# Slot starts from one product per two batches: two batches' thresholds in one tile, four moving columns, high and low parts added on VectorE

## The reference, cut to what matters

```python
edge_aggr = jnp.zeros((n, 128)).at[row].add(edge_features)       # n = 6250 nodes, 206250 edges
combined = jnp.concatenate([x, edge_aggr, global_expand], axis=-1) @ W_c + b_c
h = softplus(combined @ W1 + b1)
h = softplus(h @ W2 + b2)
out = _layernorm(x + h @ W3 + b3)
```

## Time and profile before

| what | value |
|---|---|
| median of 3 runs | 1718.69 us (1718.37 to 1723.56) |
| the profiled execution | 1720.1 us, its span 1718.3 us |
| counts and tables | 0 to about 62 us |
| main stage, first to last scatter | 67.7 to 1224.6 us |
| members stage and network | to 1718.3 us |
| PE / DVE / ACT / POOL busy, share of the span | 96% / 77% / 62% / 68% |
| granted PE clock, mean | 0.989 of full speed |

### The profile page before, as it was taken

The page is one execution under the profiler, slowest core; times in us unless marked ns, Lnnn a source line. Parts: engine busy times, 40 slices in busy tenths (PEclk is TensorE's granted clock), DMA queues, the critical chain, the costliest instruction groups (busy, mean ns, idle before and its releaser), DMA issues.

```text
span 1718.3 us, 62458 instructions
## 1 busy us (share of the span) xinstructions
PE 1658.1 (96%) x14853; PEld 1573.1 (92%) x14853; DVE 1328.6 (77%) x3884; ACT 1066.1 (62%) x3462; POOL 1166.5 (68%) x1473
## 2 busy tenths in 40 slices
PE   7899999999999999999999999999899999999985
PEld 4699999999999999999999999999799999999953
DVE  7887777777777777777777777777489898899957
ACT  1355555555555555555555555555588888888886
POOL 1477777777777777777777777777555555555536
PEclk9899999999999999999999999999899999999998
DMA  6377778777777787777777887777699999999922
GB/s 165 93 233 238 233 244 255 247 241 237 234 239 239 248 254 248 241 241 232 238 238 248 251 251 240 238 236 240 203 296 304 299 304 297 303 298 302 297 74 72
DMA packets 172834, 412.01 MB, mean 240 GB/s; under 512 B 31283, under 2 KB 46563, under 8 KB 172756
## 3 DMA queue, kind: packets, MB, share of 16 engines
q1 hardware_dynamic: 112956, 259.93, 49.3%
q0 software_dynamic: 52160, 148.16, 26.4%
q10 hardware_dynamic: 7689, 3.60, 1.2%
HBM read 234.52 MB, written 177.03 MB: 240 GB/s over the span
## 4 chain that ended last, share of the span: by engine, by line
PE 84%; DMA 3%; issue 3%; ACT 2%; POOL 2%; POOLq 1%; DVE 1%; SPq 0%; ACTq 0%; DVEq 0%
PE ps L1224 54%; PE ps L1296 21%; PE ps L1182 2%; PE ps L1195 2%; PE ps L1235 1%; DMA arena<-in_feats 1%; PE ps L1186 1%; DMA members<-buckets 1%; POOL buckets L534 1%; ACT arena L1079 1%; ACT arena L1081 1%; DMA buckets<-arena,index 1%; POOL sums L569 1%; DMA buckets<-arena,direct_at 1%; PE ps L1192 1%
## 5 line engine op out<-in xcount | busy, mean ns | idle before, releaser
L1224 PE MATMUL ps<-arena 128*120 128x129 f32 x9084 | 1045.6, 274 | 3.0 <-DVE arena L812 2.4
L1224 PEld LDWEIGHTS ps<-arena 128*120 128x120 f32 x9084 | 1019.8, 183 | 5.6 <-DVE arena L812 3.6
L534 POOL DMA_INDIRECT buckets<-arena,index x757 | 793.1, 1048 | 235.5 <-issue 149.0
L812 DVE TENSOR_SCALAR arena<-slot_no,slot_f 128x360 f32<-128x360 f16 x1514 | 554.1, 419 | 253.4 <-PE ps L1224 226.8
L1023 ACT ACTIVATE arena<-ps 120x387 f32<-120x387 f32 x757 | 373.6, 494 | 370.4 <-PE ps L1224 221.6
L1296 PE MATMUL ps<-mark,members 128*128 128x128 f32 x3648 | 413.4, 276 | 9.8 <-ACT mark L1110 7.2
L1296 PEld LDWEIGHTS ps<-mark,members 128*128 128x128 f32 x3648 | 411.1, 193 | 12.1 <-issue 10.5
L856 DVE TENSOR_SCALAR mark<-node_no,members 128x128 f32<-128x128 f16 x1368 | 363.1, 332 | 57.5 <-DMA members<-buckets 50.3
L569 POOL TENSOR_TENSOR sums<-sums,staged 128x128 f32 x456 | 225.3, 494 | 199.9 <-ACT staged L1098 102.8
L978 ACT ACTIVATE reach<-block_no,arena 128x128 f16<-128x128 f16 x806 | 316.8, 394 | 0.7 <-PE ps L1235 0.7
L1104 ACT ACTIVATE apart<-node_no,members 128x128 f32<-128x128 f16 x456 | 181.0, 397 | 35.4 <-DMA members<-buckets 25.6
(11 more groups left out here) (171 smaller groups left out, 601.7 us busy)
## 6 DMA issues: line engine op xcount, KB each, us to landing
members<-buckets SPq DMA_DIRECT2D x456, 258.0 KB, 3.6
arena<-in_feats SPq DMA_DIRECT2D x201, 516.0 KB
buckets<-sums SPq DMA_DIRECT2D x48, 258.0 KB
buckets<-arena,index POOLq DMA_INDIRECT x757
buckets<-sums SPq DMA_DIRECT2D x49, 129.0 KB
buckets<-sums SPq DMA_DIRECT2D x49, 64.5 KB
xn<-in_x ACTq DMA_DIRECT2D x1, 2800.0 KB
arena<-in_xT SPq DMA_DIRECT2D x11, 250.0 KB, 3.9
```

Of the source, the lines that this page charges most:

```text
L534: pool.indirect_dma_start(units, bass.IndirectOffsetOnAxis(ap=index[0:SLOTS, s, b:b + 1], axis=0), rows[0:SLOTS, o, :], None).then_inc(sca ...
L812: dve.tensor_scalar(perm[0:TP, b, t, :], slot_no[0:TP, :, :].rearrange("p r b -> p (r b)"), slot_f[0:TP, s, b * TPB + t:b * TPB + t + 1], ...
L1224: mm = pe.matmul(ps[0:SLOTS, MOVED + b, r * ROWF:(r + 1) * ROWF], perm[0:TP, b, t, r * SLOTS:(r + 1) * SLOTS], feat[0:TP, s, b * TPB + t, ...
```

## The change

Two batches share one `reach` tile: `border2` is taken from a product that the kernel already made for another table (`PAIRS`), with the even batch's buckets on partitions 0 to 63 and the odd batch's on 64 to 127. `goto16` gets four columns for each pair of batches: even high, even low, odd high, odd low, with zeros in the half that belongs to the other batch. PE makes one product of four columns for each pair, and because high and low parts now lie in different columns, DVE adds them (`sum_gotos`), once for each chunk, between PE and ACT's `indices`. ACT makes one tile for two batches.

```diff
-        goto16 = sb("goto16", [P, JB], f16)
+        goto16 = sb("goto16", [P, HALF, 2, 2], f16)
+        border2 = sb("border2", [P, HALF])
+        goto_f = sb("goto_f", [P, 2, CB])
-        reach = sb("reach", [P, RS, P], f16)
+        reach = sb("reach", [P, RS // 2, P], f16)
# POOL, at the start
+            pool.memset(goto16[:, :, :, :], 0.0).then_inc(goto_zeroed, 1)
# DVE, tables: one 51-column subtraction instead of two, and one memset more
+                dve.memset(tri_at16[:, ODD + KS:ODD + KS + 1], float(P)).then_inc(tables16_set, 1)
# DVE, before the loop
-            for h, part in enumerate(halves(goto16)):
-                rise = ps[:, RISE + h, 0:HALF]
-                dve.wait_ge(rise_done, h + 1)
-                dve.tensor_scalar(part, rise, 0.125, None, ALU.mult).then_inc(goto_a, 1)
-                dve.wait_ge(goto_a, 2 * h + 1)
-                dve.scalar_tensor_tensor(part[ODD:P, :], rise[ODD:P, :], 0.125, part[ODD:P, :], ALU.mult, ALU.subtract)\
-                   .then_inc(goto_a, 1)
+            rise = ps[:, RISE, 0:HALF]
+            dve.wait_ge(goto_zeroed, 1)
+            dve.wait_ge(rise_done, 1)
+            for odd in range(2):
+                own = slice(odd * ODD, (odd + 1) * ODD)
+                dve.tensor_scalar(goto16[own, :, odd, 0], rise[own, :], 0.125, None, ALU.mult).then_inc(goto_a, 1)
+            dve.wait_ge(goto_a, 2)
+            for odd in range(2):
+                own = slice(odd * ODD, (odd + 1) * ODD)
+                dve.scalar_tensor_tensor(goto16[own, :, odd, 1], rise[own, :], 0.125, goto16[own, :, odd, 0],
+                                         ALU.mult, ALU.subtract).then_inc(goto_a, 1)
+
+            def sum_gotos(c, s):
+                n = CB if not isinstance(c, int) else chunk_batches(c)
+                dve.wait_ge(reach_used, c * (CB // 2) + n // 2)
+                wait(dve, index_ready, c - 1)
+                dve.tensor_reduce(goto_f[0:SLOTS, s % 2, 0:n],
+                                  ps[0:SLOTS, GOTO + s % 2, 0:2 * n].rearrange("p (b h) -> p b h", h=2), AX.X, ALU.add)\
+                   .then_inc(goto_summed, 1)
...
             permutation(0, 0)
+            sum_gotos(0, 0)
             permutation(0, 1)
# DVE, in place(), behind the permutation
+                if b == 0 and (not last or c + 1 < CHUNKS):
+                    sum_gotos(c + 1, s + 1)
# ACT, before the loop
+            act.activation(border2[:, :], ps[:, PAIRS, 0:HALF], ACT.Copy, scale=-1.0, bias=0.5).then_inc(border2_made, 1)
# ACT, reached()
-                wait(act, reach_used, g + 1 - RS)
+                wait(act, reach_used, j + 1 - RS // 2)
-                act.activation(reach[:, r, :], block_no[:, :], ACT.Sign, bias=border[:, bass.ds(g, 1)])\
+                act.activation(reach[:, r, :], block_no[:, :], ACT.Sign, bias=border2[:, bass.ds(j, 1)])\
# ACT, indices()
-                act.wait_ge(reach_used, c * CB + n)
+                act.wait_ge(goto_summed, c + 1)
-                act.activation(index[0:SLOTS, s, 0:n], ps[0:SLOTS, GOTO + s % 2, 0:n], ACT.Identity,
+                act.activation(index[0:SLOTS, s, 0:n], goto_f[0:SLOTS, s % 2, 0:n], ACT.Identity,
# ACT, take()
-                if not ends or k + AHEAD < NBAT:
-                    reached(i * BODY + (k + AHEAD), (k + AHEAD) % RS)
+                if k % 2 == 1 and (not ends or k + AHEAD < NBAT):
+                    reached(i * (BODY // 2) + (k + AHEAD) // 2, (k + AHEAD) // 2 % (RS // 2))
# PE, before the loop: both products into one PSUM bank, DVE is told after the second
-            for h, part in enumerate(halves(count_f)):
-                pe.matmul(ps[:, RISE + h, 0:HALF], differ[0:KS, :], part[0:KS, :], start=True, stop=True)\
-                  .then_inc(rise_done, 1)
+            for odd in range(2):
+                at_ = (1 - odd) * ODD
+                mm = pe.matmul(ps[:, RISE, 0:HALF], differ[0:KS, at_:at_ + P],
+                               count_f[0:KS, :].rearrange("p (j a) -> p j a", a=2)[:, :, odd], start=(odd == 0), stop=(odd == 1))
+            mm.then_inc(rise_done, 1)
# PE, gotos()
-                wait(pe, index_ready, c - 1)
-                pe.wait_ge(reach_made, c * CB + nb)
-                for b in range(nb):
-                    pe.matmul(ps[:, GOTO + s % 2, b:b + 1], reach[:, (s * CB + b) % RS, :],
-                              goto16[:, bass.ds(c * CB + b, 1)], start=True, stop=True).then_inc(reach_used, 1)
+                wait(pe, goto_summed, c - 1)
+                pe.wait_ge(reach_made, c * (CB // 2) + nb // 2)
+                for j in range(nb // 2):
+                    pe.matmul(ps[:, GOTO + s % 2, 4 * j:4 * j + 4], reach[:, (s * (CB // 2) + j) % (RS // 2), :],
+                              goto16[:, bass.ds(c * (CB // 2) + j, 1), :, :].rearrange("p j a h -> p (j a h)"),
+                              start=True, stop=True).then_inc(reach_used, 1)
```

More of the change, by code:

```diff
@@ L55, in gnn_bucketed_edge_sum_mlp_layernorm @@
     assert (TP * TPB + K * (ROWS - 1)) // ROWS <= SLOTS <= P and ROWS * ROWF <= 512
-    assert ROWS == 3
+    assert ROWS == 3 and CB % 2 == 0 and NBAT % 2 == 0 and AHEAD % 2 == 1
     MS = 8
@@ L122, in gnn_bucketed_edge_sum_mlp_layernorm @@
         ones32 = sb("ones32", [P, P])
-        differ = sb("differ", [P, P])
+        differ = sb("differ", [P, ODD + P])
         before16 = sb("before16", [P, P], f16)
@@ L270, in gnn_bucketed_edge_sum_mlp_layernorm @@
         goto_a = sem("goto_a")
+        goto_zeroed = sem("goto_zeroed")
+        border2_made = sem("border2_made")
+        goto_summed = sem("goto_summed")
         starts_made = sem("starts_made")
@@ L626, in masks @@
                 dve.tensor_copy(tri_at16[:, ODD:ODD + KS], tri[:, 0:KS]).then_inc(tables16_set, 1)
+                dve.memset(tri_at16[:, ODD + KS:ODD + KS + 1], float(P)).then_inc(tables16_set, 1)
+                dve.tensor_tensor(differ[:, ODD:ODD + KS + 1], eye[:, 0:KS + 1], ident[:, 0:KS + 1], ALU.subtract)\
+                   .then_inc(tables16_set, 1)
                 dve.tensor_copy(ident2_16[0:K, 0, :], eye[0:K, 0:K]).then_inc(tables16_set, 1)
@@ L634, in masks @@
                     dve.memset(before16[:, at_ + KS:at_ + KS + 1], float(P)).then_inc(tables16_set, 1)
-                    dve.tensor_tensor(differ[:, at_:at_ + KS + 1], eye[:, 0:KS + 1], ident[:, 0:KS + 1], ALU.subtract)\
-                       .then_inc(tables16_set, 1)
             def mark_bucket(k):
@@ L972, in _, with reached @@
                .then_inc(boff1_made, 1)
-            def reached(g, r):
-                wait(act, reach_used, g + 1 - RS)
-                if not isinstance(g, int):
+            act.activation(border2[:, :], ps[:, PAIRS, 0:HALF], ACT.Copy, scale=-1.0, bias=0.5).then_inc(border2_made, 1)
+            def reached(j, r):
+                wait(act, reach_used, j + 1 - RS // 2)
+                if not isinstance(j, int):
                     act.nop(nofuse=True)
-                act.activation(reach[:, r, :], block_no[:, :], ACT.Sign, bias=border[:, bass.ds(g, 1)])\
+                act.activation(reach[:, r, :], block_no[:, :], ACT.Sign, bias=border2[:, bass.ds(j, 1)])\
                    .then_inc(reach_made, 1)
@@ L988, in indices @@
                         act.wait_ge(scattered[STREAMS - 1], 16 + body * 16)
-                act.activation(index[0:SLOTS, s, 0:n], ps[0:SLOTS, GOTO + s % 2, 0:n], ACT.Identity,
+                act.activation(index[0:SLOTS, s, 0:n], goto_f[0:SLOTS, s % 2, 0:n], ACT.Identity,
                                scale=4.0 * RUNITS, bias=part_row[0:SLOTS, :]).then_inc(index_ready, 1)
-            act.wait_ge(border_made, 2)
+            act.wait_ge(border2_made, 1)
             act.wait_ge(iota_set, 7)
-            for g in range(RS):
-                reached(g, g % RS)
+            for j in range(RS // 2):
+                reached(j, j)
             act.wait_ge(ends_done, 1)
@@ L1027, in _ @@
                 set_locals(0, c)
-            for g in range(RS, AHEAD):
-                reached(g, g % RS)
+            for j in range(RS // 2, (AHEAD + 1) // 2):
+                reached(j, j % (RS // 2))
             indices(0, 0, 0, 0)
```

## The result

The changed kernel takes 1730.16 us (median of 4 runs, 1729.12 to 1731.74) against 1719.91 us for the kernel before over 4 runs (1718.37 to 1723.56). The ratio is 1.0055, with a 95% interval of 1.0043 to 1.0067: 0.55% slower, and 2 us beyond the upper end of the range. The profiled execution took 1731.7 us, its span is 1729.1 us against 1718.3.

What follows compares the result with a forecast made beforehand. The prediction took POOL's back-to-back scatters, 22.93 us a body, to bound the main stage; +0.7 before the loop and -0.8 in the first bodies made -0.1 us, 1718.6 us. The range was 1706 to 1728 us.

Steps and rivals of the forecast that it cites:

- PE's saving: Main stage: 403 fewer products and weight loads save PE 0.16 us a body, nothing of the span, since POOL hides it.
- The sum: Main stage, DVE: 202 new sums of 0.2 us, 40 us in all, fit inside its waits for PE; nothing on the path.
- Rivals A and D: Main stage: A (0.10), PE sets the pace, 1686 to 1711; D (0.02), POOL waits for `index` at each chunk, 1800.
- POOL makes descriptors without a pause: Main stage: POOL's idle 0.305 us per instruction is a step, not a wait, so POOL paces bodies at 22.93 us.
- POOL's durations: Main stage: scatter times vary with DVE's phase, bounds -24 to +23 us; first bodies give -0.8, the rest is 0.
- rival C: Main stage: POOL is disturbed more, collisions of 0.53 us repeat; one in every second body adds 12, 1731 us; chance 0.16.
- The gain of 0.8: First three bodies of 138.23 to 207.83 us: PE catches up sooner and saves their excess, -0.8 us.
- ACT's order: Main stage: a chunk's last tile is made behind the row copy before the one it used to follow; worth nothing by itself.
- The companion claim: Main stage: with ACT's tile made sooner, PE no longer waits for `reach` ahead of its own next move; worth nothing.
- Before the loop: Start, DVE's four `goto16` steps: +1.0 us, +3.3 if strided writes double them; +0.7 taken into the sum.
- One memset at the start ... Nothing: Start, POOL: the added memset runs while POOL has nothing else to do and costs nothing.
- rivals B and C: Overlap of lines 812 and 534: B (0.19), POOL disturbed less, 1707 us; C (0.16), disturbed more, 1731 us.

Runs made afterwards that it cites:

- early_before: The kernel before with ACT making each `reach` tile one batch earlier (AHEAD 12 in place of 11); 1727.91 us, ratio 1.0033.
- keys_after: The changed kernel with the bucket numbers that `hot` compares against read from PSUM in place of SBUF; 1710.88 us, ratio 0.9946.
- sum_before: The kernel before with a DVE reduce of the products' bank added per chunk, result unused, ACT's `indices` waiting for it; 1720.32 us, ratio 0.9991.
- late_reach: The changed kernel with the shared `reach` tiles made one batch later, a chunk's last tile again behind the row copy; 1719.78 us, ratio 0.9993.
- keys_before: The kernel before with the bucket numbers that `hot` compares against read from PSUM in place of SBUF; 1701.36 us, ratio 0.9899.
- all_fixed: start_fixed with the bucket numbers that `hot` compares against read from PSUM; 1704.53 us, ratio 0.9896 to the kernel before.
- fixed_late: all_fixed with the shared tiles made one batch later, as in late_reach; 1707.04 us, ratio 0.9911 to the kernel before.
- fixed_pe_load: all_fixed with every slot product issued twice, the second into unused columns; 1696.77 us, ratio 0.9864 to the kernel before.
- fixed_both_load: all_fixed with every slot product issued twice and an extra unread ACT tile in even batches; 1698.57 us, ratio 0.9863 to the kernel before.
- zero_act: The changed kernel with `goto16` cleared by ACT in place of POOL's memset; 1731.43 us, ratio 1.0063 to the kernel before.
- start_fixed: The changed kernel with `goto16` cleared by ACT and stored in four planes, so DVE writes without gaps; 1728.75 us, ratio 1.0055.

## Why the prediction was wrong

**Right.** PE's saving (0.20 us a body, forecast 0.16) is hidden behind POOL: POOL's idle time is 0.305 us per instruction after as before, and nothing above 0.32 is found past 130 us. The 403 tiles fewer on ACT gain nothing by themselves. The sum is hidden; it takes 0.16 us, forecast 0.2. Members stage and network are unchanged. Rivals A and D didn't happen: POOL's pace is slower than PE's, and ACT's `index` is never late. "POOL makes descriptors without a pause" is right as far as the pause goes; what POOL does in that time no run shows. For the direct scatters of the kernel before the trace has 1.007 us of POOL each and 2.4 us (median) from issue to landing.

**The step that failed is POOL's durations**, "More I can't derive, so the rest is 0". It put the change of the scatters' durations at nothing; it was 6.5 us. The place was known in part and the outcome was written down as rival C: a repeated collision at 0.53 us, of which ten more pass the 5.2 us that count as slower. Twenty more came, 20 x 0.53 = 10.6 us; all `hot`s together took 9.5 us more from POOL and the other DMAs some 3 less. I gave C a chance of 0.16 and took no part of it into the sum. The gain of 0.8 that I expected in the first bodies was a loss instead: from the first scatter to the third body the kernel after lost another 1.1 us (4.0 to 5.0). No run isolates that part.

**Behind it, ACT's order**, "Worth nothing by itself". It was seen (the last tile moves from behind a row copy to before the one it used to follow) and costed by the work alone, with the reason that POOL sets the pace. But where POOL is disturbed depends on DVE's phase (scatters over 1.5 us had their `hot` 0.09 to 0.13 us in), and a step moved on an engine with slack shifted that phase here. early_before shows that this alone brings 38 collisions in place of 17 and costs 6 to 7.5 us in a kernel with nothing else changed. The companion claim, that PE then no longer waits for `reach`, is false as well: 12.3 us against 1.6, inside PE's slack.

**Before the loop** is the other term that failed, by size: +0.7 in the sum, +4.0 at the first scatter. For the four steps the forecast was +1.0 and the bound for strided writes +3.3. The steps start 62.11 - 60.84 = 1.27 later and take 4.32 us where before 62.07 - 60.84 = 1.23 were left on the path, in all 4.4 at the first permutation (66.43 against 62.07). The forecast had 2.22 for the four steps. Stored without gaps they take 2.43, so the chain was costed rightly and the value between the bounds was chosen wrongly: the doubling came. Of the later start, "One memset at the start ... Nothing" is the cause on average: POOL had nothing else to do, but DVE had, and 1.31 us of its first step went to the memset. I asked what POOL's path would lose, and not whom the instruction would hold. PE's clock moved along with the start, as the forecast took it: the granted clock is 0.50 from 62 to 72 us in the kernel after, 0.87 from 72 to 76 and 1.00 after, before 0.50 from 62 to 68, 0.87 from 68 to 70 and 1.00 after. By an estimate from these shares it reached 1.00 near 73.0 us, before near 68.5. Nothing of the delay came back by it.

**The reading of the earlier trace rows was wrong too.** I took the scatter's end, 0.15 us after the permutation pair, as a sign that the pair holds POOL. The pair only stands next to `hot` in DVE's order, and the place that rivals B and C name, line 812 beside line 534, is the wrong one. In the timeline of the kernel after, from 994.4 to 996 us, VectorE has nothing to do behind `hot`:

```profile
994.41 1.55 POOL L540 DMA_INDIRECT buckets<-arena,index  x1 [0.30 <-ACT arena L1048]
994.52 0.56 DVE L653 TENSOR_TENSOR hotc<-keys_k,arena 128x392 f16<-128x392 f16 x1
995.96 0.41 DVE L832 TENSOR_SCALAR arena<-slot_no,slot_f 128x360 f32<-128x360 f16 x1 [0.88 <-PE ps L1251]
```

The scatter takes 1.55 us all the same, with the next permutation only at its end; and keys_after leaves every pair in place and has no scatter above 1.19. So the scatters of 1.5 us and more go with `hot`, a VectorE `tensor_tensor`: 1.55 us in place of 1.00 with both its inputs in SBUF, 1.08 to 1.12 in keys_after at the same distance (0.12 or 0.13 us) with one of them in PSUM. Of the new sum I had said that no row shows such a reduce next to a scatter; sum_before shows one, a reduce of 0.15 us beside a scatter of 0.99.

## What to carry to other kernels

Where one engine issues back to back and sets the pace, read the spread of its instruction times before anything else: here 20 us of 1720 lay in scatters of 1.00 us that took up to 1.6, and moving one small operand of another engine into PSUM was worth 18 us, where the change took some 9 us of work (46 x 0.20) from PE and gained nothing. A change that takes work from engines with slack has two prices to look for: what its reordering does to the phase of whatever disturbs the bottleneck (6 to 7.5 us in early_before), and whom its new set-up instructions hold (1.31 us of VectorE's first step here) or how long they write (4.32 us in place of 2.43). The test for a phase effect is cheap and goes both ways, the same order change put into the old kernel and taken out of the new.

## What the runs showed of the hardware

- An indirect DMA on POOL took about 1.55 us (1.53 to 1.61) in place of 1.00 where a VectorE `tensor_tensor` with two SBUF inputs (0.56 us) began 0.12 or 0.13 us after it, in 15 of 18 cases before and 36 of 37 after; where it began at 0.07 to 0.10 the DMA took 1.01 to 1.06, but for one of 46 before and none of 56 after (4 of 65 in late_reach). With one input in PSUM the `tensor_tensor` took the same 0.55 to 0.56 us and the longest DMA was 1.21 in the six kernels built so (keys_after, keys_before, all_fixed, fixed_late, fixed_pe_load, fixed_both_load).
- Where POOL sets the pace and `hot` has two SBUF inputs, 70 to 97 of 200 `hot`s begin 0.05 to 0.15 us after an indirect DMA, where an even spread would give 15. It isn't the second SBUF input that gathers them: keys_after, with one, has 70. In the two profiles where PE sets the pace (keys_before, fixed_pe_load) there are 6 and 2. What gathers them is open.
- A POOL memset of 128 x 1616 f16 that took 1.43 us stretched a VectorE `tensor_scalar` on int32 in SBUF from 1.74 (before) to 3.05 us (after), though VectorE's began 1.18 us before it; zero_act, without the memset, has 1.66.
- VectorE writes of 404 f16 results from PSUM took 1.07 us with 8 bytes from one to the next (after) and 0.59 without gaps (start_fixed). Reading the four moving columns of a product 404 elements apart instead cost PE nothing in sight: its body in the free run is 22.18 us in start_fixed and 22.17 in the kernel after.
- The quickest kernel by the median is one whose PE does more: 1696.8 us with every slot product twice (fixed_pe_load), 1704.5 with each once (all_fixed).
